# Attention 1 of a fused two-layer kernel: a wider mask matmul, and the output bias added to X by GpSimd

## The reference

```python
m = silu(c) @ wmod                       # per batch: sa, ca, ga, sb, cb, gb
h = layernorm(x) * (1 + ca) + sa
q, k, v = h @ Wq.T, h @ Wk.T, h @ Wv.T   # 4 heads of 32
aw = where(causal, q @ k.T, lowest)      # per head, 256 x 256
attn = softmax(aw) @ v
out = g * A_mem + (1 - g) * attn         # A_mem: elu(q)+1 against a small memory
x = x + ga * (out @ Wo.T + bo)           # ga: one number per batch and feature
```

## Time and profile before

| | before |
|---|---|
| median of 3 runs | 915.63 us |
| the profiled execution's own time | 914.76 us |
| its span | 912.9 us |
| PE busy, of the span | 751.2 us (82%) |
| DVE busy | 623.3 us (68%) |
| ACT busy | 574.9 us (63%) |
| POOL busy | 326.9 us (36%) |

### The profile page before, as it was taken

One profiled execution on the slowest core, in us unless ns is written; L12 is line 12 of the kernel. 1 busy time (PEld: TensorE's weight loads), 2 busy tenths in 40 slices (PEclk: granted clock), 3 DMA queues, 4 the chain that ended last, 5 costly groups with the idle time before them and its releaser, 6 DMA issues. The chain is left out here.

```text
span 912.9 us, 17945 instructions
## 1 busy us (share of the span) xinstructions
PE 751.2 (82%) x6002; PEld 546.6 (60%) x6002; DVE 623.3 (68%) x1509; ACT 574.9 (63%) x1285; POOL 326.9 (36%) x412
## 2 busy tenths in 40 slices
PE   3466888888588874679999999589999985999996
PEld 3222444444244333579999998467777764887874
DVE  3075787787577826677777775357676855888885
ACT  0214777777477774548888887377767743555553
POOL 3541324224221000140000000367778552776674
PEclk9999999999899997779999999789999986999999
DMA  5354353443865020000000000000000070355430
GB/s 135 34 59 49 54 55 44 53 52 48 157 121 61 8 34 17 1 1 1 1 1 1 1 1 2 1 1 2 2 1 1 3 188 4 104 146 154 114 107 23
DMA packets 78221, 42.05 MB, mean 46 GB/s; under 512 B 8649, under 2 KB 76082, under 8 KB 78002
## 3 DMA queue, kind: packets, MB, share of 16 engines
q1 hardware_dynamic: 78130, 40.89, 24.4%
HBM read 25.66 MB, written 2.24 MB: 31 GB/s over the span
## 5 line engine op out<-in xcount | busy, mean ns | idle before, releaser
L563 DVE TENSOR_REDUCE att_negmax<-att_p_max 128x2 f32<-128x512 f32 x256 | 164.6, 685 | 85.0 <-PE att_p_max L443 84.1
L647 ACT ACTIVATE att_probs<-att_p_sT 128x1024 f32<-128x1024 f32 x128 | 129.3, 1021 | 56.0 <-PE att_p_sT L449 55.1
L443 PE MATMUL att_p_max<-att0p_QK 48*128 48x256 bf16 x512 | 91.9, 290 | 36.8 <-DVE att_negmax L563 12.0
L2141 POOL TENSOR_TENSOR moe_z_lo<-moe_z,moe_z_hi 128x512 fp32r<-128x512 f32 x64 | 96.7, 1523 | 54.9 <-ACT moe_z_hi L2094 54.1
L449 PE MATMUL att_p_sT<-att0p_QK 51*128 51x256 bf16 x512 | 85.6, 279 | 1.2 <-DMA att0p_QK<-att_maxT 1.2
L933 PE MATMUL ffn0s_p_h<-ffn0s_u_hi,ffn_h_hi 128*128 128x256 f32 x256 | 71.5, 313 | 18.1 <-DVE ffn0s_u_lo L1200 12.8
L443 PEld LDWEIGHTS att_p_max<-att0p_QK 48*128 48x128 bf16 x512 | 33.6, 97 | 86.8 <-DVE att_negmax L563 47.4
L472 PE MATMUL att_p_o<-att_probs,att0p_V 128*32 128x256 f32 x1024 | 70.2, 393 | 9.5 <-ACT att_probs L647 8.4
L1200 DVE TENSOR_TENSOR ffn0s_g_lo<-top_raw,ffn0s_g_hi 128x512 fp32r<-128x512 f32 x64 | 50.4, 804 | 38.4 <-ACT ffn0s_g_hi L1145 37.1
L2132 DVE TENSOR_TENSOR moe_z<-moe_act_u,top_raw 128x512 f32<-128x512 f32 x64 | 73.7, 1151 | 2.2
L729 POOL TENSOR_TENSOR att_rstd<-att_var_eps,top_minus_half 128x2 f32<-128x2 f32 x16 | 11.5, 719 | 172.3 <-DVE att_var_eps L556 172.3
(11 more groups left out here) (273 smaller groups left out, 2047.6 us busy)
## 6 DMA issues: line engine op xcount, KB each, us to landing
top_raw<-combine SPq DMA_DIRECT2D x32, 512.0 KB, 6.5
att0p_QK<-att_parts SPq DMA_DIRECT2D x192, 64.0 KB
top_X<-in_L_attn_x SPq DMA_DIRECT2D x4, 512.0 KB, 6.9
top_raw<-in_L_ffn_h_w SPq DMA_DIRECT2D x2, 1024.0 KB
out_x<-top_X SPq DMA_DIRECT2D x8, 256.0 KB, 2.3
top_wo_all<-gates SPq DMA_DIRECT2D x1, 1024.0 KB, 5.9
prep_wmod<-in_L_wmod SPq DMA_DIRECT2D x2, 384.0 KB, 3.6
top_raw<-in_L_ffn_w_w SPq DMA_DIRECT2D x3, 256.0 KB
```

The source lines that it names most:

```text
L443: mm = pe.matmul(p_max[u % 2][:, i, :], QK[r][rows, g, 0, i * P:(i + 1) * P], QK[r][rows, g, 1, :], start=True, stop=True)
L563: dve.tensor_reduce(negmax[:, :, w, g], p_max[u % 2][:], AX.X, ALU.max, negate=True).then_inc(maxed, 1)
L647: act.activation(probs[g % 2][:, t % 2], p_sT[t % 2][:], ACT.Exp).then_inc(exped, 1)
L2141: pool.tensor_tensor(z_lo[e % RING][:], z[e % RING][:], z_hi[e % RING][:].bitcast(F32), ALU.subtract).then_inc(z_lo_ready, 1)
```

## The change

The mask of a head is applied by one matmul over both diagonal blocks: its moving operand is the 128-column mask read twice, and its output is columns 0 to 127 and 256 to 383 of the head's bank. All eight score matmuls now come first and the four masks behind them. Since a `start=True` marks the whole bank, only the first query tile's matmul has it.

The one-row matmul of the output projection goes. The gated bias is made for all partitions (`gbo1_all`, for which `bo1` is loaded with a broadcast to 128 partitions), and GpSimd adds it to X of batch b right after it has normalised that batch, five steps before DVE adds the projected output. DVE's addition waits for that too.

```diff
-    loads.append((k.bo1[:], a["L1_attn_bo"].rearrange("(o d) -> o d", o=1)))
+    loads.append((k.bo1[:], a["L1_attn_bo"].rearrange("(o d) -> o d", o=1).to_broadcast([P, D])))
...
-                    pool.tensor_tensor(k.gbo1_row[:], k.wo1_all[0:1], k.bo1[:].unsqueeze(1).to_broadcast([1, B, D]), ALU.mult
+                    pool.tensor_tensor(k.gbo1_all[:], k.wo1_all[:], k.bo1[:].unsqueeze(1).to_broadcast([P, B, D]), ALU.mult
...
-            pool.memset(k.ones_row[:], 1.0)
...
                     pe.matmul(p_s[:, h, at:at + keys], q[head(h), at:at + P], ks[head(h), 0:keys],
-                              start=True, stop=False, skip_group_check=True)
-                for h in range(H1):
-                    mm = pe.matmul(p_s[:, h, at + keys - P:at + keys], k.ident16[:], k.mask16[:], start=False, stop=True,
-                                   skip_group_check=True)
+                              start=(i == 0), stop=False, skip_group_check=True)
+            for h in range(H1):
+                diagonal = p_s[:, h, :].rearrange("p (i c q) -> p i c q", i=NT, c=2)[:, :, 0, :]
+                mm = pe.matmul(diagonal, k.ident16[:], k.mask16[:].unsqueeze(1).to_broadcast([P, NT, P]), start=False,
+                               stop=True, skip_group_check=True)
             mm.then_inc(scored, 1)
...
-                pe.matmul(out, OT[b % 2][:, i * P:(i + 1) * P], k.wo1_all[:, b, :], start=True, stop=False)
-                mm = pe.matmul(out, k.ones_row[0:1, :], k.gbo1_row[0:1, b, :], start=False, stop=True)
+                mm = pe.matmul(out, OT[b % 2][:, i * P:(i + 1) * P], k.wo1_all[:, b, :], start=True, stop=True)
...
             at_least(dve, logits_made, b - 2)
+            dve.wait_ge(bias_added, b + 1)
...
             ins.then_inc(xn1_ready, 1)
+            x = k.X[:, b * NT:(b + 1) * NT, :]
+            pool.wait_ge(xn1_ready, b + 1)
+            pool.tensor_tensor(x, x, k.gbo1_all[:, b, :].unsqueeze(1).to_broadcast([P, NT, D]), ALU.add).then_inc(bias_added, 1)
```

More of the change, by code:

```diff
@@ L1433, in attention1 @@
         x_added = sem("x_added")
+        bias_added = sem("bias_added")
         hT2_ready = sem("hT2_ready")
@@ L2213, in build @@
         k.bg = sb("bg", [P, E])
-        k.bo1 = sb("bo1", [1, D])
-        k.ones_row = sb("ones_row", [1, P])
+        k.bo1 = sb("bo1", [P, D])
         k.wo1_all = sb("wo1_all", [P, B, D])
-        k.gbo1_row = sb("gbo1_row", [1, B, D])
+        k.gbo1_all = sb("gbo1_all", [P, B, D])
         k.ga_dram = nc.dram_tensor("gates", (B, D), F32, kind="Internal").ap()
```

## The result

The changed kernel takes 900.17 us (median of 4 runs, 899.47 to 903.29), the kernel before beside it 915.51 us (914.82 to 916.39). The ratio is 0.9839, with a 95% interval of 0.9814 to 0.9863: 15.3 us less, where 17.1 were forecast.

The account below looks back on a forecast made before the run. Attention 1 was taken as bound by a loop of PE's nearly continuous stream and DVE's copy. Projection and related terms of 14.1 us plus masks of 3.0 gave 17.1, so 915.63 becomes 898.5 us, range 895.5 to 904.5.

Parts of the forecast that it names:

- The loop: Attention 1: PE and DVE bound each step in turn; dropping the projection's one-row matmuls gains 1.13 us in seven periods.
- The masks: Attention 1, first score piece to maxima: 1.85 us becomes 1.64, saved 15 times, 3.0 us in all.
- m: Gain per step from the new order of scores and masks: 0.2 us, bounds -0.3 and +0.6.
- one of the two 0.24: Issue and turnaround time, 0.24 us in each of two score groups; the forecast took the middle, 0.96 for both groups.
- Rival A: The masks give nothing or cost, so the time is 901.5 to 906 us; chance 0.17.
- POOL is hidden, narrowly, and priced at zero: GpSimd's 0.81 us addition in attention 1 puts POOL 0.14 us a step behind, covered by 1.4 us of slack.
- the 0.85 us of step 14: Gain forecast for steps 12 and 14 each, whose chain goes over DVE's gate waiting for the memory product.
- rival C: DVE and POOL block each other, 0.73 us in 16 steps, 11.7 us, giving 910 us; chance 0.04.
- rival D: PE's clock falls to 1.2 GHz inside the stage, 4.9 us more a step; 928 us with six steps; chance 0.04.
- Rival B: POOL becomes the bound as the addition costs 1.2 to 1.57 us, giving 901 to 906 us; chance 0.08.
- the term of 2.4: End of attention 1: about 1.3 us arriving through POOL's scaling, plus 1.09 from the last projection.
- The small edits: Bias multiply over 128 partitions, larger `bo1` load and a dropped memset: zero, within 0.5 us both ways.

Follow-up runs that it names:

- e2: Changed kernel without its mask part: only the bias is in the new form, scores and masks as before; 904.11 us, 0.9864 of the kernel before.
- e1: Changed kernel without its bias part: only scores and masks are in the new form, bias still by one-row matmuls; 911.72 us, 0.9947 of the kernel before.
- e3: Changed kernel without GpSimd's bias addition and DVE's wait for it, so the gated bias is missing from its output; 899.53 us.
- e4: Changed kernel with the rounding copy of the router's input moved from POOL to ScalarE; 896.9 us, 0.9783 of the kernel before.
- e10: The code of e4 run again beside a run of the changed kernel; 899.42 us, against 900.64 for that changed kernel.
- e5: Changed kernel with DVE taking the reciprocals of batch 12's second half before the router's ranking in step 12, not after it; 899.04 us.
- e6: Changed kernel with the edits of e4 and e5, the ranking spread over two steps and the weighing one step later; 899.83 us.
- e12: Changed kernel with thirteen of the ranking's fourteen comparisons in step 12 left out; 896.93 us, 0.978 of the kernel before.
- e11: Changed kernel with POOL making the bias addition twice per batch, once into a spare tile; 906.99 us, 6.35 more than the changed kernel beside it.
- e8: Kernel before with only the wide load of `bo1` to 128 partitions, otherwise computing as before; 916.15 us against 916.25.

## Why the prediction came out as it did

**The loop.** Right. PE's continuous stream through masks, transposes, projection and DVE's copy was the bound, and both savings arrived in each steady period. The projection's four pieces cost 0.44 us (0.47 forecast) and e2 puts the part at 1.12 us a period (1.13 forecast); it was limited, as said, by DVE's chain of maxima, addition and copy. PE's 0.39 us of idle time ahead of the memory product is the place where that shows (forecast 0.4).

**The masks.** Right, and sized too small: m is 1.85 - 1.51 = 0.34 us a step where I had taken 0.2, from bounds of -0.3 and +0.6. The row that was lacking: four masks of 256 columns go in 664.52 - 664.08 = 0.44 us, against 0.33 for 128 columns. With the way to DVE they take 664.72 - 664.08 = 0.64, close to the 0.68 forecast. The larger part of the miss is the scores: both groups together take 664.08 - 663.21 = 0.87 where I had taken 0.96, nearly the 0.84 at which one of the two 0.24 goes whole. Rival A falls by this row and by e1.

**POOL.** The total was right, and this is the step within it that failed: "POOL is hidden, narrowly, and priced at zero". The first half holds only until step 11: up to there e3 has the same 7.92. The arrears were taken as 0.14 us a step from POOL's work of 8.17. Measured, the round is 8.14 to 8.26 us (699.09 - 633.38 over eight steps gives 8.21) and the period 7.92 rather than 8.03, so 0.29 a step, 2.3 in eight, against a slack of 1.4. In step 12 POOL's addition, split and scaling have come to lie beside DVE's normalisation and ranking, and DVE's instructions take 1.3 us longer: shown by e3, e4 and e10. Of the 0.15 us a step that I was short, 0.04 is POOL's work and 0.11 the loop, which became faster than I thought.

**Step 12 and step 13.** I gave step 12 the 0.85 us of step 14, and without POOL's arrears most of it arrives: in e3 the step takes 10.13, 0.72 less than before. What took it back are the 1.29 us above, which the prediction had as rival C, for another step and by another path: DVE and POOL in each other's way. Where DVE has idle time, in the steady steps, this costs nothing; where it runs without a gap, in step 12, it costs all of it. In step 13 the faster loop brings PE to its transposes 2.6 us ahead of the scaling that hangs on the ranking. This wait was in no term, and e5, e6 and e12 show that the ranking is its cause, by two paths; but it costs nothing by itself. What costs is PE's clock, which falls for some microseconds: rival D in small, priced at a whole stage by me and real in one step (9.86 us against 7.69 in e12). Why it falls there is open, since it falls in e1 without that wait and stays up in e2 with one of 1.60. Rival B is what e11 builds, and the changed kernel isn't it.

**The tail.** The gain is 3.92 where 2.4 was forecast. The clock holds longer at its end in this pair of profiles: in step 16 the transposes L1499 take 0.66 us where they took 1.05. But in e8, whose attention 1 is that of before, these transposes take 0.64 as well, and against its tail of 21.22 the gain is 2.75. So 1.17 of the excess belongs to the one execution that was profiled before, and the term of 2.4 was close.

**Why the total was near.** The excess in the steady steps (1.45), the tail (1.5) and the start (0.3) pays for what steps 12 and 13 lost (3.5), and of that excess 1.2 is the long tail of the profile before. The closeness of 16.9 to 17.1 is in part luck. The small edits and the new wait of DVE cost nothing to be seen: the addition L1774 follows the maxima at once, and e8 clears the load.

## What to carry to other kernels

Work put on a side engine is hidden only against the period that the change itself makes; work out its arrears a step with that period, add them up to the next step that is unlike the others, and ask what shares that engine's time there. When a loop gets faster, look at the one long item that sits on another engine (here a ranking whose comparisons alone take 2.6 us): it was covered by the slower loop, and what is queued behind it may hold the fast one by more than one path. Before cutting a path, look whether the engine with the long item is itself idle anywhere up to the next round: DVE was not, so freeing PE in e5 gained nothing. And take two profiles of the same code before a microsecond in one stretch is explained: the tail's 1.2 us were the execution's.

## What the runs showed of the hardware

In the projection, four pieces with one-row weights among four with full-size weights cost 1.12 us more than the four alone (1.56 against 0.44), more than four full pieces would. Four masks of 256 columns in place of eight of 128 save 0.34 us a step with the same columns in all; the return to 32-row pieces between two groups of masks goes with it. DVE's fourteen comparisons of 128x112 take 2.00 us without POOL's scaling beside them and 2.62 with it, and its normalisation of two 128x128 tiles 0.78 and 1.22. After a PE wait of 2.6 us, at full clock ahead of it, the four transposes behind it took 1.11 us in place of 0.66 for the same line in the step before; after a wait of 1.60 (e2) the clock stayed at 1.00, and after gaps of 0.26 and 0.55 (e1) it fell.
